# Four PSUM banks of ScalarE: one shared ring, or three for scores and one for small results

## The reference, cut to what matters

```
x = x + attn_rope(layernorm(x))     # layer 0 "rope": rotated q, k and v
x = x + ffn(layernorm(x))           # layer 1 "ffn"
x = x + attn_cov(layernorm(x))      # layer 2 "cov": scores of centred q and k, and their variances
x = x + ffn(layernorm(x))           # layer 3 "ffn"

def ffn(x):
    h = x + attention(layer_norm(x))          # 16 heads, softmax(q k^T / sqrt(8)) v, then w_o
    t = layer_norm(h)                         # 2048 tokens
    probs = softmax(t @ w_gate); tw, ti = top_k(probs, 2); tw /= sum(tw)
    out = sum over e of we[:, None] * (gelu(t @ w1[e] + b1[e]) @ w2[e] + b2[e])
    return h + out
```

## Time and profile before

| | before |
|---|---|
| median of 3 runs | 1042.02 us |
| profiled execution, its time | 1043.29 us |
| its span | 1041.3 us |
| mean granted TensorE clock | 0.959 of full speed |
| TensorE busy | 991.2 us, 95% |
| ScalarE busy | 604.9 us, 58% |
| VectorE busy | 558.0 us, 54% |
| GpSimd busy | 395.4 us, 38% |

### The profile page before, as it was taken

The page is one execution under the profiler, slowest core; times in us unless marked ns, Lnnn a source line. Parts: engine busy times, 40 slices in busy tenths (PEclk is TensorE's granted clock), DMA queues, the critical chain, the costliest instruction groups (busy, mean ns, idle before and its releaser), DMA issues.

```text
span 1041.3 us, 22226 instructions
## 1 busy us (share of the span) xinstructions
PE 991.2 (95%) x8516; PEld 745.7 (72%) x8516; DVE 558.0 (54%) x1427; ACT 604.9 (58%) x1128; POOL 395.4 (38%) x839
## 2 busy tenths in 40 slices
PE   3999999999999999999999999899999999999998
PEld 2655555666655999999886555566665699999997
DVE  4877777788884212122336788678888322111111
ACT  1356666887887454444445777688777744444443
POOL 6858676757743100012022353736873310000000
PEclk9677888999999999999999999899999999999999
DMA  8000000000000000000000000000000000000000
GB/s 286 2 2 2 3 2 2 3 3 3 3 3 2 1 1 1 2 1 1 1 2 1 3 3 2 3 3 3 3 2 3 2 2 4 8 1 11 1 11 11
DMA packets 9960, 10.42 MB, mean 10 GB/s; under 512 B 1528, under 2 KB 7552, under 8 KB 9856
## 3 DMA queue, kind: packets, MB, share of 16 engines
q1 hardware_dynamic: 8848, 7.64, 2.3%
q10 hardware_dynamic: 1008, 1.38, 0.4%
HBM read 7.44 MB, written 1.05 MB: 8 GB/s over the span
## 4 chain that ended last, share of the span: by engine, by line
PE 79%; DVE 15%; POOL 3%; issue 3%; ACT 0%; DMA 0%; DVEq 0%; ACTq 0%; POOLq 0%
PE bankR L625 22%; PE bankO L387 11%; PE bankE L406 8%; DVE M L986 7%; PE bankE L360 6%; PE bankE L614 6%; PE bankE L616 6%; PE bankE L615 6%; PE bankE L397 2%; DVE QKV L948 2%; PE bankR L373 2%; PE bankR L457 1%; PE bankR L427 1%; PE bankR L475 1%; PE bankE L467 1%
## 5 line engine op out<-in xcount | busy, mean ns | idle before, releaser
L986 DVE TENSOR_REDUCE M<-bankR 128x2 f32<-128x512 f32 x512 | 326.6, 684 | 97.2 <-PE bankR L373 95.9
L741 ACT ACTIVATE Pr<-bankE 128x512 f32<-128x512 f32 x512 | 277.5, 595 | 132.7 <-PE bankE L360 128.9
L845 ACT ACTIVATE Pr<-bankE,b1c 128x512 f32<-128x512 f32 x256 | 171.8, 689 | 176.1 <-PE bankE L616 175.0
L1141 DVE SCALAR_TENSOR_TENSOR X<-bankR,WE,X 128x128 f32<-128x128 f32 x256 | 72.1, 344 | 332.7 <-PE bankR L625 332.7
L625 PEld LDWEIGHTS bankR<-w,Pr 128*128 128x128 f32 x2048 | 238.3, 192 | 6.3 <-issue 1.1
L625 PE MATMUL bankR<-w,Pr 128*128 128x128 f32 x2048 | 238.8, 275 | 0.9 <-DVE X L1141 0.9
L373 PE MATMUL bankR<-KQ 32*128 32x256 f32 x1024 | 170.1, 346 | 6.6 <-DVE M L986 4.5
L387 PE MATMUL bankO<-Pr,Vx 128*32 128x256 f32 x2048 | 173.0, 413 | 0.6 <-ACT OT L733 0.5
L360 PEld LDWEIGHTS bankE<-KQ 32*128 32x128 f32 x1024 | 81.8, 194 | 101.5 <-issue 64.3
L360 PE MATMUL bankE<-KQ 32*128 32x256 f32 x1024 | 136.1, 343 | 0.0
L373 PEld LDWEIGHTS bankR<-KQ 32*128 32x128 f32 x1024 | 108.8, 197 | 16.2 <-DVE M L986 11.7
(11 more groups left out here) (166 smaller groups left out, 1185.7 us busy)
## 6 DMA issues: line engine op xcount, KB each, us to landing
THL<-in_w SPq DMA_DIRECT2D x1, 2048.0 KB, 8.9
KQ<-MT SPq DMA_DIRECT2D x128, 4.0 KB
X<-in_x SPq DMA_DIRECT2D x8, 128.0 KB, 6.6
out_x<-X SPq DMA_DIRECT2D x4, 256.0 KB, 2.3
ropeA<-in_ropeA ACTq DMA_DIRECT2D x1, 384.0 KB, 5.2
ropeB<-in_ropeB ACTq DMA_DIRECT2D x1, 384.0 KB, 5.5
w_lo_rope<-in_w_qkv_rope ACTq DMA_DIRECT2D x1, 192.0 KB, 2.9
b_qkv_rope<-in_b_qkv_rope ACTq DMA_DIRECT2D x1, 192.0 KB, 4.3
```

Of the source, the lines that this page charges most:

```text
L741: nc.scalar.activation(Pr[:, (h // HG) % 2, h % HG], act_bank("S", layer, b, h).rearrange("p (k q) -> p k q", k=TT), ACT.Exp, scale=EXP_SC ...
L845: nc.scalar.activation(G[:, e % 2, c, :], act_bank("hid", ph, at, c), ACT.Gelu_apprx_tanh, bias=b1c[:, e * FC + c:e * FC + c + 1]).then_in ...
L986: v.tensor_reduce(M[:, b % 2, :, h], dve_bank("raw", layer, b, h).rearrange("p (t k) -> p t k", t=TT), AX.X, ALU.max, negate=True).then_in ...
L1141: v.scalar_tensor_tensor(xt[:, j, t, :], dve_bank("out", ph, at)[:, t * D:t * D + D], WE[:, j * BT + t, e:e + 1], xt[:, j, t, :], ALU.mult ...
```

## The change

The ring of four banks is cut in two: `ring_e` with three banks for the transposed scores and the experts' first products, and `ring_s` with one bank for all small results. `act_bank` looks a key up in one ring or the other.

```diff
         def act_bank(*key):
-            return bankE[:, ring_e.place[key]].rearrange("p k q -> p (k q)")
+            n = ring_e.place[key] if key in ring_e.place else HG - 1 + ring_s.place[key]
+            return bankE[:, n].rearrange("p k q -> p (k q)")
...
-        ring_e, ring_r = Ring(HG), Ring(3)
+        ring_e, ring_s, ring_r = Ring(HG - 1), Ring(1), Ring(3)
...
             def do_mT(layer, b, half):
                 need(pe, maxed, layer, b, NP * half + NP)
-                ring_e.take(pe, ("mT", layer, b, half))
+                ring_s.take(pe, ("mT", layer, b, half))
...
-                ring_e.give(("mT", layer, b, half), mT_copied, layer, b, half + 1)
+                ring_s.give(("mT", layer, b, half), mT_copied, layer, b, half + 1)
...
             def stack_turn(name, t, layer, b, src, event):
-                ring_e.take(pe, (name, layer, b, t))
+                ring_s.take(pe, (name, layer, b, t))
...
                 for t in range(TT):
                     stack_turn("K", t, layer, b, Kst, kT)
-                    ring_e.give(("K", layer, b, t), kT_copied, layer, b, t + 1)
+                    ring_s.give(("K", layer, b, t), kT_copied, layer, b, t + 1)
```

More of the change, by code:

```diff
@@ L409, in do_zT @@
                 need(pe, z_ready, layer, b)
-                ring_e.take(pe, ("zT", layer, b))
+                ring_s.take(pe, ("zT", layer, b))
                 for x in range(2):
@@ L414, in do_zT @@
                 k.then_inc(zT.sem, 1)
-                ring_e.give(("zT", layer, b), zT_copied, layer, b)
+                ring_s.give(("zT", layer, b), zT_copied, layer, b)
             def do_proj(layer, b):
@@ L448, in do_qT @@
                     stack_turn("Q", t, layer, b, Qst, qT)
-                    ring_e.give(("Q", layer, b, t), qT_copied, layer, b, t + 1)
+                    ring_s.give(("Q", layer, b, t), qT_copied, layer, b, t + 1)
             def do_outT(layer, b):
@@ L463, in do_onT @@
                 need(pe, unroped_sum if rope else divided, layer, b)
-                ring_e.take(pe, ("onT", layer, b))
+                ring_s.take(pe, ("onT", layer, b))
                 src = O1[:].rearrange("p t h x -> p t (h x)") if rope else On
@@ L468, in do_onT @@
                 k.then_inc(onT.sem, 1)
-                ring_e.give(("onT", layer, b), onT_copied, layer, b)
+                ring_s.give(("onT", layer, b), onT_copied, layer, b)
             def do_wo(layer, b):
@@ L482, in do_uT @@
                     need(pe, u_ready, layer, b, 8)
-                    ring_e.take(pe, ("uT", layer, b))
+                    ring_s.take(pe, ("uT", layer, b))
                     for x in range(2):
@@ L487, in do_uT @@
                     k.then_inc(uT.sem, 1)
-                    ring_e.give(("uT", layer, b), uT_copied, layer, b)
+                    ring_s.give(("uT", layer, b), uT_copied, layer, b)
             def do_gate(layer, b):
@@ L631, in do_weT @@
                 need(pe, gated, ph, j)
-                ring_e.take(pe, ("weT", ph, j))
+                ring_s.take(pe, ("weT", ph, j))
                 for t in range(BT):
@@ L635, in do_weT @@
                 k.then_inc(weT.sem, 1)
-                ring_e.give(("weT", ph, j), weT_copied, ph, j)
+                ring_s.give(("weT", ph, j), weT_copied, ph, j)
             def do_b2(ph, j):
```

## The result

| | before | after |
|---|---|---|
| median | 1041.86 us (4 runs) | 1219.91 us (4 runs, 1217.52 to 1222.58) |
| span of the profiled execution | 1041.3 us | 1220.5 us |
| TensorE busy | 991.2 us | 1095.4 us |
| the rest of the span | 50.1 us | 125.1 us |
| mean granted clock | 0.959 | 0.875 |

The ratio is 1.171, with a 95% interval from 1.168 to 1.174. The forecast was 1157 us with a range up to 1205: the direction was right, the size too small, and the time lies above the range. The last row is worked out: the clock has two levels, so the time at 1.2 GHz is 2 x (1 - mean clock) x span. It is that of the profiled execution.

A forecast was written before the change was run, and what follows sets the result against it. TensorE, busy 95% of the span, was taken as the bound. 1043.3 + 89.1 us of waits + 26 us of clock falls = 1158.4, or 1157 us against the median; forecast's own range 1125 to 1190, widened to 1105 to 1205.

The forecast's parts named there:

- Step (7): Granted clock in attention steps: falls in every second of 26 steps, 13 x 2.0 = 26 us; ends 0 and 130 us.
- rival B: Clock stays low through nearly all attention steps, 26 steps at 5 us of loss: 1220 to 1260 us; chance 0.08.
- Steps (1) to (4): TensorE waits for copies: second K, Q groups 51.2 us, turns after onT 31.6, mT 5.1, between experts 1.2; together 89.1.
- Step (5): Transposed scores with three banks in turn: no wait for exponentials added, and nothing gained from not waiting for small results.
- Step (6): Experts' first products in three banks: fourth chunk's bank is free 0.41 us early, so nothing; without that cover at most 44 us.
- A: Stalls at K and Q turns mostly absorbed by shorter later waits, clock stays: 1087 us; chance 0.12.
- C: Something else already holds the second groups, and waits only change their names: 1042 us; chance 0.02.
- D: Faster: 36.3 us of score weight loads held by exponentials could come back, down to 1006 us; chance 0.03.

The follow-up runs named there:

- the run with filled waits: Changed kernel plus matmuls nobody reads ahead of each second K and Q group and the first group behind onT; 1134.9 us, 1.089 to before.
- the run with second groups and onT out: Changed kernel with the second K and Q groups and onT put back into the ring of the scores; 1049.7 us, 1.0065 to before.

## Why the prediction was wrong

**Step (7), the clock, failed.** It said: 13 falls at 2.0 us, 26 us. Measured are 220 us more at the half clock and 104.2 us more of busy time, and the run with filled waits gives 85 us of it back. The mechanism was the right one: idle time close together brought the clock down in steps that had kept it. Both factors of the term were too small. I counted a fall in every second of 26 steps, 13; there are 19 more stretches, 29 against 10. And I priced one at 4.0 us, the shorter of the two seen in the earlier trace rows; the mean is 10.5 us. In the same rows stood a fall of 10 us, and it was the better price: 19 more stretches of 10.5 us are 200 us at half. One error went the other way: I reckoned half of the time at the half clock as lost, and by the filled waits it was 0.34 of it. The term's upper end, 130 us, held the measured 85 to 104. The range stopped at 1205 because I gave rival B 0.08; B's lower end, 1220, is what came.

By the rule cited from the Trainium skill (TensorE: Matmul & The Clock Gate, "A second HAM failure mode: psum-queue depth-cycling") the clock oscillates when banks are cycled with short idle times between. The trace agrees, with 29 stretches and no idle time of TensorE over 1.04 us in the steps of the layers behind the first. The number of new stretches, 19, lies between the 13 that I took and the 26 that I gave this rule.

**Steps (1) to (4), the waits themselves, were right.** 89 us were forecast; 75 us are listed, and the run with filled waits is 93 us above before. The counts fit too: 66 waits for copies of K and Q, 26 behind onT, 18 of mT. In the example step, the second K group comes 1.37 us after the first (forecast 1.34), the second Q group 1.34. The wait behind onT is listed with 1.01 us, and by the starts it is 268.25 against 267.10 for a group that follows onT by 0.27 us, 1.15 us (forecast 1.23). mT waits 0.21 (0.23). The step grew by 3.35 us (3.06).

**Step (5) was right**: scores gained and lost nothing, 0.0 us of idle time. **Step (6)** put the experts at nothing; it is 2.9 us in four waits, and 5.3 us by the starts in the run with second groups and onT out.

**The rivals.** A (absorbed) is refuted: the time is far above 1087, and VectorE's waits for raw scores grew from 95.9 to 260.1 us, so it had no backlog to make up. C and D are refuted by the two new rows in the list of waits. B gave the number, and its condition came about in part: nearly every step of both pipelines has a fall, but the clock is at half for some four tenths of their time (0.78 from 30 to 390 us, 0.81 from 620 to 960), and not through nearly all of it.

## What to carry to other kernels

A producer that writes two results in a row needs two buffers, however small they are: with one, the price here was the whole round of turns, copy and release (1.34 us) less the turns themselves (0.54 us). Count every such wait by the starts of the instructions, and then ask what the clock makes of them together; here 75 us of waits cost 178. When a granted clock already falls in the trace, price a further fall by the mean length of all that are seen (8.5 us here), not by the shortest. And compare clocks over several executions: that of one profile can be off by as much as the effect that is looked for.

## What was not expected of the hardware

In the layers behind the first the clock fell to 1.2 GHz in nearly every step, though TensorE never idled for longer than 1.04 us at a time in them and was busy for 86% of the time from 30 to 390 us. Matmuls without use in the waits brought it back to 2.4 GHz, from 305 to 54 us at the half clock, and made the kernel 85 us faster without shortening one wait. Half as many did nearly as much (75 us at half, 1140.4 us). By what rule idle time is counted stays open: less idle time goes with less half clock in these runs, but not in proportion.
